# A four-layer graph network on one core: first edge-weight product over all 128 rows, and the edge network's first product one group earlier in two layers

## The reference

```python
h = silu(edge_scalars @ fc_w1)              # 16 (layer 0) or 8 inputs -> 64 hidden
w = h @ fc_w2                               # 64 -> 192 weights per edge
s, v = x[:, :64] @ l0, x[:, 64:] @ l1       # node features, scalar and vector part
m0a = w[:, :64] * s[src] * sh0
m1a = (w[:, 64:128] * s[src])[..., None] * sh1
m1b = w[:, 128:160, None] * v[src] * sh0
m0b = w[:, 160:192] * dot(v[src], sh1)
agg = segment_sum(concat(m0a, m0b, m1a, m1b), dst)
x   = layernorm(x + f(agg @ ..., x @ ...))
```

## Time and profile before

| what | us |
|---|---|
| median of 3 runs | 4392.32 (4391.31, 4392.32, 4588.6) |
| the profiled execution | 4397.57, with a span of 4395.8 |
| busy in the span | PE 3382.7, DVE 3296.0, POOL 3185.6, ACT 2472.2 |
| edge stage of layer 0 | about 110 to 700 of the span |
| edge stage of layer 2 | about 2540 to 3060 |
| edge stage of layer 3 | about 3450 to 3965 |

### The profile page before, as it was taken

The page is one execution under the profiler, slowest core; times in us unless marked ns, Lnnn a source line. Parts: engine busy times, 40 slices in busy tenths (PEclk is TensorE's granted clock), DMA queues, the critical chain, the costliest instruction groups (busy, mean ns, idle before and its releaser), DMA issues. The chain is left out here.

```text
span 4395.8 us, 72815 instructions
## 1 busy us (share of the span) xinstructions
PE 3382.7 (77%) x13920; PEld 1659.6 (38%) x13920; DVE 3296.0 (75%) x8785; ACT 2472.2 (56%) x7452; POOL 3185.6 (72%) x3110
## 2 busy tenths in 40 slices
PE   0888887995999999999930088887997888886676
PEld 0333334662444434444410033332665333334554
DVE  1677767994888888888868746564999556658999
ACT  0333335995555555555537745554999444435777
POOL 1577777996788888888636667775787677766887
PEclk9898898997999999999965589998999899988998
DMA  9322226995455455555459923232998222226786
GB/s 382 116 75 76 74 77 211 318 317 136 117 128 130 120 132 121 128 129 120 115 168 371 355 73 82 81 82 75 317 326 281 73 78 78 77 69 205 240 241 201
DMA packets 582482, 713.96 MB, mean 162 GB/s; under 512 B 77680, under 2 KB 407734, under 8 KB 582130
## 3 DMA queue, kind: packets, MB, share of 16 engines
q1 hardware_dynamic: 491446, 533.50, 40.6%
q0 software_dynamic: 84672, 141.06, 12.0%
q10 hardware_dynamic: 6268, 38.40, 2.1%
HBM read 484.47 MB, written 244.35 MB: 166 GB/s over the span
## 5 line engine op out<-in xcount | busy, mean ns | idle before, releaser
L564 POOL DMA_INDIRECT aggregates<-agg_out,scatter_index x588 | 589.9, 1003 | 324.4 <-issue 183.0
L1329 ACT ACTIVATE y_chunk<-residual,ln_minus_mean_rstd,ln_rstd 128x160 f32<-128x160 f32 x1568 | 700.9, 548 | 76.0 <-DMA x_layer<-y_chunk 55.5
L1398 POOL TENSOR_TENSOR ln_rstd<-ln_var_eps,minus_half 128x4 f32<-128x4 f32 x392 | 497.5, 1269 | 108.6 <-ACT ln_var_eps L1338 73.1
L552 POOL DMA_INDIRECT gathered<-x_layer,gather_index x392 | 394.2, 1006 | 132.0 <-issue 114.2
L1293 PE MATMUL psum<-self_weights,x_chunk_T 128*128 128x160 f32 (+1 forms) x2352 | 429.2, 328 | 58.1 <-ACT x_chunk_T L1352 54.3
L644 PE MATMUL psum<-identity,scaled_x 128*128 128x128 f32 x588 | 152.8, 296 | 384.4 <-ACT scaled_x L598 359.2
L1504 DVE BATCH_NORM_STATS2 ln_stats<-residual 128x6 f32<-128x160 f32 x1568 | 396.2, 309 | 6.8
L709 DVE COPY gather_index<-src_index 128x4 int32 (+1 forms) x147 | 25.4, 173 | 496.4 <-DMA gathered<-x_layer,gather_index 372.8
L1293 PEld LDWEIGHTS psum<-self_weights,x_chunk_T 128*128 128x128 f32 x2352 | 359.7, 197 | 94.1 <-ACT x_chunk_T L1352 53.4
L552 POOL DMA_INDIRECT gathered<-in_x,gather_index x196 | 212.8, 1086 | 153.1 <-ACT scaled_x L598 63.2
L880 POOL DMA_INDIRECT aggregates<-agg_out,last_index x196 | 234.5, 1196 | 114.5 <-issue 62.8
(11 more groups left out here) (231 smaller groups left out, 10449.4 us busy)
## 6 DMA issues: line engine op xcount, KB each, us to landing
x_layer<-y_chunk SPq DMA_DIRECT2D x294, 320.0 KB, 4.7
x_chunk<-x_layer SPq DMA_DIRECT2D x294, 320.0 KB, 4.6
agg_chunk<-aggregates SPq DMA_DIRECT2D x196, 320.0 KB, 5.4
sh_rows<-in_sh_big SPq DMA_DIRECT2D x49, 768.0 KB, 8.5
agg_chunk<-aggregates SPq DMA_DIRECT2D x98, 384.0 KB, 5.7
aggregates<-zero_rows ACTq DMA_DIRECT2D x1, 36864.0 KB
x_chunk<-in_x SPq DMA_DIRECT2D x98, 322.0 KB, 3.8
agg_chunk<-aggregates SPq DMA_DIRECT2D x98, 322.0 KB, 3.8
```

Source lines behind the costliest of these rows:

```text
L552: eng.indirect_dma_start(gathered[:, par, b, 0:width], None, x_table[l][:, :], bass.IndirectOffsetOnAxis(idx_src[:, par, b:b + 1], 0))\
L564: eng.indirect_dma_start(agg_table[:, :], bass.IndirectOffsetOnAxis(idx_last[:, q, b:b + 1], 0), agg_out[:, q, b, :], None, bounds_check=N ...
L1329: op = eng.activation(y_out[:, buf, b, :], res[:, buf, b, :], ACT.Identity, bias=shift[:, buf, b:b + 1], scale=rstd[:, buf, b:b + 1])
L1398: eng.tensor_tensor(rstd[:, buf, :], var_eps[:, q, :], minus_half[:, 0:T], ALU.pow)\
```

## The change

Two edits in `edge_tensor`. The first weight product takes all 128 rows of `W1` and `hid` in place of rows 0 to 63; the added rows of `W1` are zeros. In layers 2 and 3 the edge network's first product is that of group `s` instead of `s-1`, and its place is behind the feature products instead of in front of the output product; in layer 0 it stays. It is now a function `hidden`, so lines below shift: L656 becomes L639, L671 and L672 become L673 and L674, L675 and L676 become L677 and L678, L683 and L685 become L687 and L689.

```diff
+            def hidden(g, q):
+                wait(eng, S["attr1"] if q else S["attr0"], (g - q) * 16 + 32)
+                wait(eng, S["hidden"], g)
+                eng.matmul(bank(H), W(l, "F1")[0:C["K"], :], attr_t[0:C["K"], q, :], start=True, stop=True)\
+                   .then_inc(S["hidden_mm"], 1)
...
-                if live(s, 1, NG):
-                    g, q = s - 1, 1 - par
-                    wait(eng, S["attr1"] if q else S["attr0"], (g - q) * 16 + 32)
-                    wait(eng, S["hidden"], g)
-                    eng.matmul(bank(H), W(l, "F1")[0:C["K"], :], attr_t[0:C["K"], q, :], start=True, stop=True)\
-                       .then_inc(S["hidden_mm"], 1)
+                if l == 0 and live(s, 1, NG):
+                    hidden(s - 1, 1 - par)
...
-                    eng.matmul(bank(W1), W(l, "W1")[0:64, :], hid[0:64, :], start=True, stop=True)
+                    eng.matmul(bank(W1), W(l, "W1"), hid[:, :], start=True, stop=True)
                     eng.matmul(bank(W2), W(l, "W2")[64:128, :], hid[64:128, :], start=True, stop=True)\
                        .then_inc(S["w_mm"], 1)
                     wait(eng, S["products"], g)
                     eng.matmul(bank(E1), W(l, "E1"), xt1[:, :], start=True, stop=True)
                     eng.matmul(bank(E2), W(l, "E2"), xt2[:, :], start=True, stop=True).then_inc(S["e_mm"], 1)
+                if l and live(s, 0, NG):
+                    hidden(s, par)
```

## The result

The change made the kernel slower, by about 1%. Four runs gave 4425.9, 4433.48, 4439.95 and 10361.36 us, a median of 4436.72; the four of the kernel before have a median of 4393.17. The run of 10361.36 us (mean clock 0.324) and one of 4588.6 us of the kernel before are slow ones: both medians still count them, the ratio doesn't. It is 1.0095, with a 95% interval of 1.0075 to 1.0115. The forecast was 4360, and its range ended at 4408.

A forecast was written before the change was run, and what follows sets the result against it. POOL's pace was taken to bound the edge stages, with time lost to PE gaps of about two microseconds. 4397.6 + 0 + 12 - 44 = 4365.6, about 4360 us as the runs' median is 5.3 lower; range 4318 to 4408.

The forecast's parts named there:

- What bounds the kernel: Edge stages: POOL sets the pace and waits only for `agg_out`; PE gaps of about two microseconds cost time, not PE's work.
- Part 1: First weight product on 128 rows, 147 groups: +1.03 us a step, 151 us of PE time, direct cost taken as 0.
- rival (d): All three layers: the wide product isn't covered by PE's gap, 151 us paid on top, 4511 us; chance 0.03.
- Part 2: Edge network's first product moved, layers 2 and 3: waits for this step's DMAs, transposes 1.0 us late, cost 12 us.
- the two-step round trip: Layers 2 and 3: from gathers to the gathers after next spans two steps, so each pays half the excess.
- excess 0.25: Layers 2 and 3: lateness of the transposes beyond the free 0.75 us; 0.12 a step, 98 groups, 12 us.
- Part 3: Edge stages of layers 0, 2 and 3: fuller PE gaps stop clock drops and POOL's waits; gain 44 us.
- Rival (a): Layers 2 and 3: the wait for the rows becomes the bound; +78 us at 4.1 landing, 4426 us; chance 0.12.
- the ring: Layers 2 and 3: moved product, transposes back, output product, L737 and DMAs; 7.18 us plus landing, decides above 3.1 landing.
- the cover: Layer 2: `agg_out` is ready 1.68 us before POOL takes it, of which 0.75 us is free.
- Rival (b): Edge stages: the clock doesn't recover, as drops come from the kind of PE work; 4404 us; chance 0.10.
- Rival (c): Layers 0 and 3: more comes back than POOL's waits; 4330 us, or 4315 if layer 3 follows; chance 0.13.

The follow-up runs named there:

- e5: Kernel before with the edge network's first product moved and the attributes' DMA issued early on its own semaphore, weight products still paired on 64 rows; 4371.88 us, ratio 0.9952.
- e1: Kernel before with only the first weight product widened to 128 rows; 4371.85 us, ratio 0.9962.
- e14: Changed kernel with the vector message in PSUM and an unused product of constants ahead of the wait for rows in layers 2 and 3; 4385.61 us, ratio 0.9982.
- e2: Kernel before with only the edge network's first product moved in layers 2 and 3, first weight product on 64 rows; 4444.05 us, ratio 1.0123.
- e8: Changed kernel with the vector message written to PSUM in place of SBUF; 4401.63 us, ratio 1.0018.
- the serial pair: Kernel before with the second weight product also on rows 0 to 63, so the two products run one behind the other; 4382.74 us, ratio 0.9987.
- the filler, e15: Kernel before with one unused 128x512 product of constants added behind L676 in all three layers; 4376.5 us, ratio 0.9966.
- e7: Changed kernel with the attributes' DMA issued early on its own semaphore and the vector message in PSUM; 4338.96 us, ratio 0.9892.
- e16: Kernel before with only the vector message written to PSUM in place of SBUF; 4348.18 us, ratio 0.9902.
- e10: The same kernel as e15, run on another chip against the kernel before there; ratio 1.0001.

## Why the prediction was wrong, point by point

- **What bounds the kernel** was right for the kernel before: POOL's pace, with `agg_out` as what it waits for. Its sentence that a gap of about two microseconds on PE is what costs time holds only for PE's old order: e5 keeps the gaps and the low clock in layer 3 and has e1's step.
- **Part 1 costs 0 on the path**: right. e1 is faster, not slower, and rival (d) falls with it. The pair takes 2.01 us (forecast 2.09).
- **Part 2, the chain**: right in each link. Landing 2.52 to 2.65 (2.5), the product ahead of the transposes 1.05 (1.04), transposes 3.57 after L344's issue (3.5) and 1.05 later than before (1.0), halving by the two-step round trip (e14). The fixed time plus bytes from the Trainium skill ("DMA: Bandwidth & Descriptors", Anatomy of one DMA) gave an estimate of 2.5 us for the 192 KB. The trace agrees (2.52 and 2.65), though these DMAs go by SP's queue.
- **The step that failed** is the term "excess 0.25, each pays half: 0.12 x 98 = 12". Part 2 alone cost 56 us in place of 12 (e2): 0.59 a step in layer 2 and 0.27 in layer 3 of its profiled execution. In quiet steps the wait is about 0.24 a step (e14), twice the 0.12. And the term counted only waiting: in layer 2 nearly half of the 0.79 that POOL's step grew by between 2610 and 3030 is not waiting at all but POOL's longer instructions (gathers 1.042 for 0.973), and part of the waiting goes with TensorE at 1.2 GHz in the lengthened steps (e8 against e14). I costed one undisturbed step, and such a step did come out as costed, with a wait of 0.55; the delayed kernel settled into steps of 11.6 with a wait of up to 2.17, followed by shorter ones.
- **Part 3, the clock**: the sign was right and the size wrong. Forecast were 44 us: 25 in layer 0, 17 in layer 3, 2 in layer 2. The wide product alone gave 10, 5 and 20 in layers 0, 2 and 3 of its profiled execution and 16 in the median; that execution is 7 us below its own median, and that of the kernel before 5 above. In e1 the waits for `agg_out` fell as forecast in layer 3 (30.1 to 14.0) and less in layer 0 (28.2 to 18.4). With part 2 in, the second error is "layer 2 from 1.6 to 0.5, layer 3 from 1.9 to 0.9": these gaps hold for an unchanged pace. The wait in front of L639 is 0.55 in a quiet step but up to 2.17 in a lengthened one, time at 1.2 GHz in layer 2 went from 7 to 40 us, and in layer 3 the waits for `agg_out` stayed at 23.4.
- **The two terms make up the miss.** Part 2 cost 56 and not 12, part 1 gave 16 and not 44. Put into the sum, 4360 + 44 + 28 = 4432; the middle one of the first three runs is 4433.
- **Rival (a)** named the right mechanism, the wait for the rows, and its time of 4426 is that of the profiled execution, but for another reason. It took the ring to decide only from a landing of 3.1 us; the landing was 2.5, and layer 2's step rose all the same. (The ring's 0.07 us from PE to L737 stands in no row; where L737 waits for PE, it starts 0.14 behind it as a rule, which changes nothing here.) Its 0.12 was low, since the forecast's own chain had already used up the cover, by 0.25. Whether the ring or that cover sets the steps of 11.6 us, no run separates.
- **Rival (b)** is refuted in layer 3: work in the gap brings the clock back, be it the wide product, the serial pair or a filler (.91 to .98 or .99). In layer 0 it isn't: the filler and the serial pair left PEclk at .92 and .90, the wide product alone brought it to .95.
- **Rival (c)** was right as mechanism and wrong in sign here. The rule, from the Trainium skill ("GPSIMD Engine Reference", Specifications), that POOL shares its memory interface with a DVE instruction of two SBUF inputs, is borne out: gathers of layer 0 at 1104 ns, 963 with one input moved to PSUM. As the rival said, the stretch stayed in layer 0 (1100 before, 1104 after); in layer 2 it grew.
- **Not explained**: 11.8 us of the profiled loss lie outside the scans of the three stages, in pieces of up to 5.6 us; e1 and e2 have pieces of up to 4 of either sign. Layer 1's edge stage, which no kernel here changes, takes 1142 to 1152 us from its first scan to its last over all traces (1144.1 before, 1150.4 after), so a piece of that size is no sign of the change. In e2 the median lost 56 us and the profiled execution 40.

The best version measured is e7: the product moved, the attributes' DMA issued early on its own semaphore, the wide product, and the message in PSUM. It runs 52 us faster than the kernel before (0.9892) on that chip. e16, one edit of the scan's input, has 41 of these.

## What to carry to other kernels

When an instruction is moved to a place where it waits, look at the semaphore and not only at the data: here the product needed 16 KB and waited for 192 KB on the same count. If the sum shows that the slack in front of the bottleneck is used up, don't price the excess from one quiet step; the lengthened steps bring stretched instructions and clock drops with them, which here made 0.6 us a step out of some 0.3. And before trusting a gain of 1%, run it on more than one chip.

## What the runs showed of the hardware that was not expected

- A gather that POOL began 0.1 to 0.9 us into a vector scan with two inputs in SBUF ended 2.04 to 2.09 us after the scan's start, whatever its own start (161 cases in the two kernels), so it occupied POOL for up to 1.99 us in place of 0.94 to 1.01; one begun just ahead of the scan was not held. With one input in PSUM the mean of layer 0 fell from 1104 to 963 ns.
- A 128x512 product of constants that nobody reads made the kernel 0.3% faster on one chip (e15), and not on another (e10, 1.0001).
- TensorE at 1.2 GHz for 51 of 420 us cost nothing where the chain had slack (e5); where it had none, the same 51 us went with 0.26 us a step (e8 against e14, which differ by a filler).
- Two of the four chips on which the experiments ran executed the kernel before 8% slower, with waits of up to 15.8 us behind PE's signals, and turned the ranking of the PSUM versions round.
